# Writing out every loop of a routed convolution block: one pass, one turn at a time, on all five engines

## The reference

```python
x_proj = jnp.einsum('bchw,oc->bohw', x, proj_w)
att1 = _route(x_proj, att1_w, att1_b, [dw1_w3, dw1_w5], [dw1_b3, dw1_b5], 1)
att2 = _route(att1, att2_w, att2_b, [dw2_w7, dw2_w9, dw2_w11], [dw2_b7, dw2_b9, dw2_b11], DIL2)
out = jnp.concatenate([att1, att2], axis=1)
...
att = jax.nn.sigmoid(att + sp_b[None, :, None, None])
gate = att[:, 0:1] + att[:, 1:2]
return out * gate + x
```

## Time and profile before

| | |
|---|---|
| median of 3 runs | 6509.45 us (6501.57 to 6514.16) |
| profiled execution, time | 6496.81 us |
| profiled execution, span | 6495.1 us |
| TensorE (matmul) busy | 4863.1 us, 75% |
| VectorE busy | 3131.1 us, 48% |
| ScalarE busy | 2138.7 us, 33% |
| mean granted TensorE clock | 0.844 |
| DMA | 1396.05 MB, mean 215 GB/s |

### The profile page before, as it was taken

The page is one execution under the profiler, slowest core; times in us unless marked ns, Lnnn a source line. Parts: engine busy times, 40 slices in busy tenths (PEclk is TensorE's granted clock), DMA queues, the critical chain, the costliest instruction groups (busy, mean ns, idle before and its releaser), DMA issues.

```text
span 6495.1 us, 160891 instructions
## 1 busy us (share of the span) xinstructions
PE 4863.1 (75%) x62816; PEld 3336.9 (51%) x62816; DVE 3131.1 (48%) x3835; ACT 2138.7 (33%) x4354; POOL 1279.7 (20%) x2006
## 2 busy tenths in 40 slices
PE   3659888787878788787878878787787878785542
PEld 1326465465646455464745546474554647464442
DVE  2042636454554654465454445545454554645263
ACT  2224334251424324142433415243341524331210
POOL 3001011211212121221212121121212112121214
PEclk9879899897989889798988979898897988886665
DMA  8885586969789696968869696887959688795657
GB/s 214 255 236 170 163 208 195 259 190 257 208 230 249 182 253 182 255 205 237 238 192 251 182 257 205 233 232 200 250 182 252 205 231 232 199 241 154 174 145 194
DMA packets 1044178, 1396.05 MB, mean 215 GB/s; under 512 B 666476, under 2 KB 877805, under 8 KB 1012701
## 3 DMA queue, kind: packets, MB, share of 16 engines
q1 hardware_dynamic: 872012, 595.02, 38.2%
q0 software_dynamic: 90416, 561.75, 27.3%
q10 hardware_dynamic: 81314, 234.18, 12.3%
HBM read 1055.02 MB, written 480.03 MB: 236 GB/s over the span
## 4 chain that ended last, share of the span: by engine, by line
DMA 37%; PE 34%; DVE 10%; issue 8%; SPq 5%; POOL 3%; ACT 1%; ACTq 1%; POOLq 0%; DVEq 0%; another core or an unknown queue 0%
DMA out_dram<-RX 18%; PE psC L913 12%; DMA RX<-w_d 8%; DMA RX<-in_x_dram 8%; PE psA L851 5%; PE psA L852 5%; DVE M2a L1118 5%; PE psA L786 4%; PE psB L882 2%; PE psB L795 2%; DVE M L1118 2%; PE psB L861 2%; DMA RX<-nat_d 2%; SPq L415 1%; PE psB L892 1%
## 5 line engine op out<-in xcount | busy, mean ns | idle before, releaser
L913 PE MATMUL psC<-RX 61*60 61x120 f32 (+7 forms) x49152 | 1447.0, 265 | 209.8 <-POOL RX L559 76.5
L913 PEld LDWEIGHTS psC<-RX 61*60 61x60 f32 x49152 | 1384.6, 132 | 280.3 <-issue 277.5
L683 ACT ACTIVATE X<-psA,bias 128x246 f32<-128x246 f32 x1024 | 639.8, 739 | 2340.7 <-PE psA L852 2340.7
L851 PE MATMUL psA<-X,RX 128*128 128x240 f32 x2048 | 1027.4, 591 | 247.1 <-DMA RX<-w_d 246.6
L852 PE MATMUL psA<-X,RX 128*128 128x240 f32 x2048 | 1013.0, 583 | 0.0
L786 PE MATMUL psA<-RX,projt 128*64 128x512 f32 x1920 | 570.1, 678 | 234.9 <-DMA RX<-in_x_dram 194.8
L851 PEld LDWEIGHTS psA<-X,RX 128*128 128x128 f32 x2048 | 471.0, 241 | 529.3 <-issue 337.2
L882 PE MATMUL psB<-ident,L 124*128 124x124 f32 x2160 | 434.8, 348 | 389.2 <-DVE RX L1192 334.6
L1206 DVE TENSOR_TENSOR RX<-RX,G 80x1280 f32<-80x1280 f32 x256 | 378.5, 1483 | 691.9 <-DMA RX<-nat_d 684.0
L1118 DVE TENSOR_REDUCE M2a<-L 124x135 f32<-124x6480 f32 x64 | 394.1, 6220 | 652.1 <-ACT L L713 652.1
L559 POOL COPY RX<-RX 64x720 f32<-64x720 f32 x512 | 398.1, 782 | 1477.3 <-DMA RX<-w_d 1476.6
(11 more groups left out here) (106 smaller groups left out, 3481.5 us busy)
## 6 DMA issues: line engine op xcount, KB each, us to landing
RX<-in_x_dram POOLq DMA_DIRECT2D x64, 2560.0 KB, 11.0
RX<-w_d ACTq DMA_DIRECT2D x256, 512.0 KB, 8.6
RX<-nat_d POOLq DMA_DIRECT2D x256, 400.0 KB, 7.8
RX<-in_x_dram POOLq DMA_DIRECT2D x512, 200.0 KB, 6.2
out_dram<-RX POOLq DMA_DIRECT2D x512, 200.0 KB, 6.0
RX<-w_d ACTq DMA_DIRECT2D x512, 180.0 KB
RX<-in_x_dram SPq DMA_DIRECT2D x128, 720.0 KB, 11.9
out_dram<-RX SPq DMA_DIRECT2D x128, 720.0 KB, 14.3
```

The costliest lines, as they stand in the source:

```text
L683: ins = nc.scalar.activation(X[:, :, :, c:c + 1].rearrange("p b t c -> p (b t c)"), psA[p][:, ch * N1:(ch + 1) * N1], ACT.Identity, bias=b ...
L851: nc.tensor.matmul(o[:, :, 0:T1], w1t[g % 2][:, cc, 0:128], rhs, start=True, stop=False, skip_group_check=True)
L913: ins = nc.tensor.matmul(o[:, :, 0:kk, a:b], w2t[2 * q + p][rows, ch, z:z + PB], src[rows, 2 * p + ch, 0:nf, 3 * cg + dc:3 * cg + dc + kk, ...
```

## The change

`repeat` calls its body for each pass, and `samples` its body for each of the 19 turns; both hardware loops are gone on all engines. What each engine computes, in which order, which tiles it uses and what it waits for stay. The program becomes longer, all waits compare with constants and all addresses are constants.

```diff
@@ -251,11 +251,8 @@
 
         def repeat(eng, lo, hi, body, written=0):
 
-            for i in range(lo, min(lo + written, hi)):
+            for i in range(lo, hi):
                 body(i)
-            if lo + written < hi:
-                with eng.Fori(lo + written, hi) as i:
-                    body(i)
 
         class Turn:
 
@@ -273,11 +270,7 @@
 
         def samples(eng, body):
 
-            for s in range(4):
-                body(Turn(s))
-            with eng.Fori(4, B - 1) as s:
-                body(Turn(s))
-            for s in range(B - 1, B + 3):
+            for s in range(B + 3):
                 body(Turn(s))
 
         def neg_step(ap, count):
```

## The result

The changed kernel takes 6703.49 us (median of 4 runs, 6696.44 to 6722.26) against 6511.81 (6501.57 to 6525.12). The ratio is 1.0298, with a 95% interval of 1.0269 to 1.0327: 192 us slower. The prediction was 6655 us in a range of 6550 to 6830, slower.

The account below looks back on a forecast made before the run. No one engine is full, but conv2 on TensorE sets the turn's time. Conv2 +200, turn branches -38, pass branches -5, registers -10 give +147 on the 6509 us median: 6655 us, range 6550 to 6830.

Parts of the forecast that it names:

- A packet of new code every 128 matmuls, and the engine asks one ahead: TensorE in conv2: written-out passes wait for each packet, requested on entering the one before; 1.1 us late at DMA share 0.88.
- The size for conv2: Conv2 in turns 2 to 14: 114 us against 99.3 to 102, +14 us a turn; all conv2s +200 us.
- Packets with idle DMA engines: Conv2's last passes, DMA idle: price per packet about 0, so 2.7 passes at 10.7 us without stalls.
- Packets beside the strip copies: Conv2 passes at DMA share 0.99: +3 us for four packets, priced between 1.1 and 3.5 us each.
- The clock in general: Conv2 pass 1 of turn 9: some 1.5 us of half clock, within its 18 us.
- one of the signs of being wrong: Clock in conv2 falling well below 0.95 would mean the stalls cost more than their length.
- The savings: Whole kernel: turn branches -38 us, pass branches -5, registers and conv1 -10.
- the 10 us taken for registers: Conv1's stage: waits and addresses become constants, -10 us taken; -40 to -75 if the whole difference were registers and branches.
- The pass branches' -5: Borders between conv2 passes: pass loop's branch gone, worth -14 us at the most, -5 taken.
- code comes in time: Rival: straight code flows without stalls, conv2 passes 1 to 7 take 10.7 us, only savings left; about 6420 us, chance 0.07.
- dearer packets: Rival: packets cost as beside x loads for the busy 82 us, conv2 129 us, 6890 us; above 6790, chance 0.12.
- Absorbed: Rival: later stages wait less for DMA; half of conv2's loss absorbed, 6556 us; between 6520 and 6570, chance 0.09.

Follow-up runs that it names:

- the pair without strip copies: Changed kernel, and the kernel with turns written out and passes looped, both without the copies from nat_d to strip_d: 6560.49 us and 6426.95 us.

## Why the prediction was right

**A packet of new code every 128 matmuls, and the engine asks one ahead.** Right. 505 packets were forecast as some 500, and the runs, their idle time of 0.5 to 1 us in the middle of conv2, and the seat of the loss in TensorE's own program are as described. That it asks one ahead is shown by the packets' times in turn 16. The kernels with bodies of one, two and four passes show that what costs is new code, and not the place of a pass.

**The size for conv2.** +14 us a turn was forecast, +18.1 came; over all conv2s +200 against +271. Three terms were mis-sized.
- Packets with idle DMA engines: priced at 0, from turn 16's pass 0. The table gives 12.0 us for passes 6 and 7 in place of 10.8 for pass 7 before, 0.4 us a packet, and turn 16 grew by 5.2 us where nothing was expected. Its extra 2.85 us are the low clock, as I took them: the granted clock was at its half level for its first 5.9 us. But so it ran that part slower, packets had more time to come, and the lead lasted beyond the pass; it could not show the price at full speed. Its 384 matmuls in one run were true and did not say what I took from them.
- Packets beside the strip copies: I put in +3 us. Pass 4 takes 19.7 us against 14.2, +5.5. Part of that is the clock: runs of 5.3 us behind idle times of 2.2 and 2.9 us.
- The clock in general: I counted 1.5 us of it, in pass 1 only. The page has 94 us more busy time of the same matmuls, 5.9 us a turn, about a third of the loss. The granted clock in conv2 fell from 0.96 to 0.90 in turn 9, which was one of the signs of being wrong: the stalls cost more than their length. This overlaps with the two terms above.
Pass 1 was priced too high (18, measured 15.3), and passes 2 and 3 a little (14.2, measured 13.7), which made up for some of it; this part is luck.

**The savings.** -53 us were forecast. Between the conv2s of turns 3 to 15 the trace has -43.5, of which the 10 turn branches at 3.8 us are 38: right. Conv1's stage showed nothing that can be called a gain, so that the 10 us taken for registers have no seat there. The pass branches' -5 is lost in conv2's sum. In the kernel with the turns alone written out the savings are 58 us.

**The sum.** +147 against a median difference of 192: the mechanism was right, and the error is conv2's size. Of the rivals, "code comes in time" is out by the runs, and "dearer packets" was true for pass 4 alone. "Absorbed" did not happen to the half, but it did to a small part. Between before and changed it can't be seen, since the profiled difference is conv2's and the branches' to 2 us. Between the kernel with the turns alone written out and the changed one the 16 conv2s grow by 292 us and the medians by 254, and one wait in between got shorter: TensorE's for VectorE's maps (L803 and L800) fell from 62.4 to 46.6 us, and in the pair without strip copies from 74.6 to 40.4. This fits that the two loops' parts (+216) came out above the whole (+192), a difference that is not clear of noise by itself.

## What to carry to other kernels

Before writing out a loop on TensorE, see how fast it runs through its program. A new packet came here every 3.96 us in the mean with little DMA work, and every 7.3 us beside the strip copies (median of pass 4); its code (some 127 matmuls with their weight loads) was used up in 3.5, so that it cost time at every packet. A loop whose body the engine holds (3 packets always, 6 in 14 conv2s of 16, 12 never) costs 0.2 us a branch. Write out the outer loop, whose branch goes to code that is no longer held (3.5 us), and keep the inner one: here 0.9911 against 1.0298 for both. The sign of it in a profile is idle time named "issue" at equal distances, and the packets of the instruction queue.

## What was not expected of the hardware

Held code in a body of two passes shows that the engine can keep 6.2 packets for going back, and yet straight code is asked for only one packet ahead, so that it stalls even with DMA share 0.08 to 0.24 (0.3 to 0.7 us a packet). The Trainium skill (Runtime: NRT & Kernel Launch, Instruction fetch mechanics) speaks of a border cost that is mostly hidden, and of full unrolling as the better choice; for TensorE at conv2's pace the runs say the opposite, 0.4 us at the least and over 2 us beside copies, and 274 us in all for the passes alone. For the turns, whose branch is dear, its advice holds: writing them out gained 58 us. Its account of a branch out of the held window agrees with 3511 and 3529 ns here. And behind idle times of 2.1 to 2.9 us in turn 9 the granted clock was at its half level for a part of the next run.
